# Attention and convolution on one core: the step that turns and scales the next group's minima, at the end of unit 6 in place of the head of unit 7

## The reference

```
q, k, v = t @ Wq.T + bq, t @ Wk.T + bk, t @ Wv.T + bv        # t: (8, 1024, 512), normalised
q, k, v = (z.reshape(B * NUM_HEADS, S, hd) for z in (q, k, v))
scores = einsum('gqd,gkd->gqk', q, k) / sqrt(hd)
wv = einsum('gqk,gkd->gqd', softmax(scores), v)
x = x + wv                                                   # layer 0
x = x + conv3x3(relu(_gn(x) * mask), weight) + bias          # layer 1
```

## Time and profile before

| | |
|---|---|
| median of 3 runs | 2764.5 us (2763.74 to 2767.18) |
| profiled execution | 2762.23 us |
| its span | 2760.4 us |
| mean granted clock of TensorE | 0.976 |
| busy in the span | TensorE 2575.8 us (93%), VectorE 2090.1 (76%), ScalarE 1086.2 (39%), GpSimd 1164.1 (42%) |

### The profile page before, as it was taken

How to read it: one execution, slowest core, us unless ns; L and a number is a source line. 1 busy time by engine, 2 the same in 40 slices (tenths; PEclk the granted TensorE clock), 3 DMA queues, 4 the chain that set the end, 5 groups by cost and what they waited for, 6 DMA issues and landing times.

```text
span 2760.4 us, 39733 instructions
## 1 busy us (share of the span) xinstructions
PE 2575.8 (93%) x11312; PEld 1002.7 (36%) x11312; DVE 2090.1 (76%) x2832; ACT 1086.2 (39%) x1801; POOL 1164.1 (42%) x907
## 2 busy tenths in 40 slices
PE   5989999998999999999899999987599999999998
PEld 2333333333333333333333333322144444444443
DVE  5787788778678778877877877779768968968714
ACT  3444435444454544455444355435323122122100
POOL 3445546655645655565555455564801103003000
PEclk9999999999999999999999999998799999999999
DMA  4233143242433315233331532421154554653524
GB/s 134 67 94 98 46 124 90 61 123 58 107 79 82 101 49 133 69 94 85 90 108 26 143 90 62 118 92 67 62 211 159 181 206 162 233 182 134 198 95 165
DMA packets 209777, 309.10 MB, mean 112 GB/s; under 512 B 80272, under 2 KB 129552, under 8 KB 209552
## 3 DMA queue, kind: packets, MB, share of 16 engines
q1 hardware_dynamic: 209552, 306.36, 36.5%
HBM read 202.88 MB, written 52.69 MB: 93 GB/s over the span
## 4 chain that ended last, share of the span: by engine, by line
PE 77%; DVE 11%; issue 5%; DMA 2%; ACT 2%; POOL 2%; DVEq 0%; SPq 0%; ACTq 0%; POOLq 0%
PE bank L747 27%; PE bank L657 14%; PE bank L602 12%; PE bank L645 11%; PE bank L620 6%; PE bank L612 4%; DVE nmax L1139 3%; DVE prob_sum L1133 2%; PE bank L634 2%; DMA q_b<-shift 1%; DVE val L1156 1%; ACT xn_hi L809 1%; POOL prob_sum L983 1%; DVE nt L209 1%; PE bank L628 0%
## 5 line engine op out<-in xcount | busy, mean ns | idle before, releaser
L1139 DVE TENSOR_REDUCE nmax<-bank 128x1 f32<-128x512 f32 x1024 | 661.2, 683 | 224.6 <-PE bank L620 217.3
L829 ACT ACTIVATE prob<-bank 128x512 f32<-128x512 f32 x1024 | 554.9, 594 | 691.6 <-PE bank L645 665.2
L747 PE MATMUL bank<-v,u_slab 128*128 128x512 f16 x3456 | 749.8, 380 | 3.4 <-DVE v L1307 3.4
L983 POOL TENSOR_TENSOR prob_sum<-prob_sum,prob 128x512 f32<-128x512 f32 x384 | 553.6, 1442 | 439.7 <-ACT prob L829 438.2
L657 PE MATMUL bank<-prob,val 128*64 128x512 f32 x2048 | 520.6, 628 | 2.3 <-ACT prob L829 2.3
L747 PEld LDWEIGHTS bank<-v,u_slab 128*128 128x128 f16 x3456 | 338.8, 98 | 413.4 <-DVE v L1307 5.1
L620 PE MATMUL bank<-k_a,q_a 128*128 128x512 f16 x1024 | 393.6, 388 | 43.8 <-DVE nmax L1139 28.8
L1133 DVE TENSOR_TENSOR prob_sum<-prob_sum,prob 128x512 f32<-128x512 f32 x384 | 380.6, 991 | 24.6 <-DVE shift L1149 16.8
L645 PE MATMUL bank<-q_a,k_a 128*128 128x512 f16 x1024 | 320.6, 385 | 41.3 <-ACT prob L829 40.4
L645 PE MATMUL bank<-q_b,k_b 128*128 128x512 f16 x1024 | 312.2, 387 | 21.3 <-DMA q_b<-shift 21.2
L1034 POOL TENSOR_TENSOR t_a<-tab_mem 128x1224 f32<-128x1224 f32 x16 | 50.1, 3131 | 447.3 <-DVEq L1256 435.0
(11 more groups left out here) (119 smaller groups left out, 2649.2 us busy)
## 6 DMA issues: line engine op xcount, KB each, us to landing
u_slab<-u_scratch SPq DMA_DIRECT2D x72, 1024.0 KB, 5.0
tile<-x_scratch SPq DMA_DIRECT2D x34, 1024.0 KB, 7.5
xs<-x SPq DMA_DIRECT2D x28, 1024.0 KB, 5.8
u_scratch<-u_w SPq DMA_DIRECT2D x96, 192.0 KB, 2.2
q_a<-qk_hi SPq DMA_DIRECT2D x64, 256.0 KB, 5.6
den_sb<-recip_scratch SPq DMA_DIRECT2D x128, 128.0 KB, 2.9
x_scratch<-xr SPq DMA_DIRECT2D x16, 1024.0 KB, 4.9
xr<-x SPq DMA_DIRECT2D x15, 1024.0 KB, 8.7
```

The source lines that it names most:

```text
L747: mm = pe.matmul(bank_at(pos, co)[:].rearrange("p (i n) -> p i n", i=2), slab[:, l, c, co * P:(co + 1) * P], image[v][:, 2 * c:2 * c + 2, ...
L829: act.activation(prob[:, (2 * u + e) % 8], sc_bank[bank_turn(s * 16 + 2 * u + e, 16 * HPI)[0]][:], ACT.Exp, scale=float(D) ** -0.5).then_i ...
L983: nc.gpsimd.tensor_tensor(acc, in0, prob[:, (2 * kc + 1) % 8], ALU.add).then_inc(s1["sum1"], 1)
L1139: dve.tensor_reduce(nmax[:, m // 2, m % 2:m % 2 + 1], src[:], AX.X, ALU.max, negate=True)\
```

## The change

The shift item is moved from place "a" of unit 7 to place "d" of unit 6, ahead of a statistics item if there is one. Both engines and the ring's order follow, since they read the same function; nothing is added or left out.

```
@@ -99,10 +99,10 @@
     tiles = [("max", first + k) for k in range(MAX_QUOTA[u])] if nxt else []
     at = {"a": tiles[0:1], "b": tiles[1:2], "c": tiles[2:]}
     at["d"] = [("value", u // 2)] if v_units and u % 2 else []
+    if nxt and u == UNITS - 2:
+        at["d"].append(("shift", 0))
     if u in stat:
         at["d"].append(("stat", stat.index(u)))
-    if nxt and u == UNITS - 1:
-        at["a"].append(("shift", 0))
     if prev and u == 2:
         at["d"].append(("den", 0))
     return at
```

## The result

The changed kernel takes 2756.49 us in the median (2753.76 to 2761.62), beside 2764.99 for the kernel before (eight runs each). The ratio is 0.9977, with an interval from 0.9967 to 0.9986: about 6.4 us faster, 3.9 to 9.1. The two medians lie 8.5 us apart, inside this interval. The sum of the prediction gave 15.4 us. The time lies inside the predicted range, but the sum is 2.4 times the 6.4 us and 1.8 times the 8.5.

A forecast was written before the change was run, and what follows sets the result against it. Stage 1 was taken as a TensorE stream with a few holes. Gains of 22.1 and 0.65 us less a loss of 7.4 gave 15.4 us off, a median of 2749 us; range 2738 to 2761.

The forecast's parts named there:

- Part 1, slot 2: Slot 2, images 0 to 6: shift ahead of the statistics item ends TensorE's waits; gain 3.16 us per image, 22.1 in all.
- Bounds 1.5 and 2.6: Slot 2's smaller gains per image: 2.6 us if VectorE's chain ends 0.6 later, 1.5 if TensorE's short pieces run at low clock.
- rival (b): Slot 2 gains only 2.6 to 1.5 us per image, 2753 to 2761 us; chance 0.15 up to 2759, beyond it 0.10 shared.
- Right behind 3.1 us of idleness: Slot 2 before the change: granted clock 0.50 from 642.20 to 645.60, following TensorE's waits of 1.76 and 1.32 us.
- Part 2, the wait of slot 7: Slot 7: the shift matmul's wait for the minima holds the value matmuls; loss 1.05 us per image, 7.4 in all.
- Rival (a): Slot 7's stall is taken up by waits TensorE already has there; 2742 us, chance 0.16.
- the clock behind slot 7's wait: Slot 7: no clock fall was put in the sum; with one, 1.7 us more, a bound of 2.75 per image.
- rival (c): Slot 7's stall takes the clock down, 1.7 us more per image; 2761 us, chance 0.10 shared with the smallest slot 2 gains.
- I leave it out of the sum: Low-clock stretches, such as behind slot 3, might be met or missed as phase shifts; some us better or worse, counted as nothing.
- Part 3: Other queues and last image: nothing, except about 0.65 us gained in the last image's slot 5.
- the 5.28 us: Last image, slot 6: TensorE's wait for its row goes, but GpSimd's masks set the end; between 0 and 5, taken as 0.
- (d): Slower: slot 7's wait outweighs slot 2's gain, losing 2.75 against 1.46 us per image with both clocks falling; 2773 us, chance 0.05.

The follow-up runs named there:

- slot 7 alone: Kernel before, with the shift at the end of unit 6 only in slot 7 of images 0 to 6: 2777.61 us, ratio 1.0047.
- the last image alone: Kernel before, with the shift at the end of unit 6 in the last image only: 2763.05 us, ratio 0.9998.
- the filled run: For slot 7: changed kernel, six unread matmuls in its wait, 2746.06 us. For slot 4: changed kernel without slot 7's move, eight in its wait, 2731.22 us.
- cut in two: Changed kernel, but in slot 7 four of the eight value matmuls go ahead of the shift matmul and four behind: 2742.65 us, ratio 0.9918.
- absent: Kernel before, with the shift at the end of unit 6 in all slots but slot 7: 2740.27 us; in slot 2 of images 0 to 6 only: 2741.7 us.
- not filled: Kernel before, with the shift at the end of unit 6 in all slots but slot 7, run again on the slot 4 filling's chip: 2742.55 us.

## Why the prediction was wrong

**Part 1, slot 2, was right.** Forecast -3.16 us per image, measured -3.36 for slots 2 and 3 together. What becomes late next is what was named: VectorE, with six maxima in a row; the first of the six comes 10.53 us behind the start of GpSimd's L989 (631.11 to 641.64), where it was 13.76. The statistics did take to the old end whatever their start: L204 takes 0.51 us instead of 1.00, since it starts later, and the three behind it 1.18 or 1.19 us. GpSimd in the same stretch of the changed kernel:

```profile
631.11 1.27 POOL L989 TENSOR_TENSOR den_sb<-pv_sb,den_sb 128x512 f32<-128x512 f32 x1 [3.44 <-DMA den_sb<-recip_scratch]
632.34 1.26 POOL L983 TENSOR_TENSOR prob_sum<-prob_sum,prob 128x512 f32<-128x512 f32 x1
633.56 1.27 POOL L996 TENSOR_TENSOR xr<-xr,den_sb 128x512 f32<-128x512 f32 x1
634.79 1.26 POOL L983 TENSOR_TENSOR prob_sum<-prob_sum,prob 128x512 f32<-128x512 f32 x1
```

These four operations end at 632.38, 633.60, 634.83 and 636.05; the four held operations of VectorE end at 632.40, 633.63, 634.84 and 636.07. Behind the last of them the same operations take 0.16 us. The Trainium skill (SBUF — State Buffer, "SBUF: two separate sides") calls the port pair that the two engines share an exclusive lock that is held for the whole instruction, on VectorE's side by operations with two inputs in SBUF or in a mode that uses both ports. The trace agrees for L209 and L211; in which mode L204 and L206, with one input, ran is shown nowhere. Bounds 1.5 and 2.6 and with them rival (b) didn't happen: TensorE's short pieces from 639.7 on kept the full clock.

But the size of this gain leans on the old kernel's clock, and here the prediction had luck in its sample. "Right behind 3.1 us of idleness" wasn't a law: in two runs that leave slot 2 as it was (slot 7 alone, the last image alone), the clock stays at full speed behind that pair of waits in 5 of 14 images. TensorE in image 2 of the run with slot 7 alone, and the stretch behind (L622 is a maximum's matmul, L659 the value matmuls):

```profile
647.54 0.39 PE L622 MATMUL bank<-k_a,q_a 128*128 128x512 f16 x1 [1.57 <-DVEq L1154]
649.25 0.61 PE L647 MATMUL bank<-q_b,k_b 128*128 128x512 f16 x2 [1.32 <-DMA q_b<-shift]
649.78 1.94 PE L659 MATMUL bank<-prob,val 128*64 128x512 f32 x8
649.20:652.60 3.40, 3.35 (x15) 1.08 (x16) 2.41 (x4) 1.69 (x3) 0.00 (x0) 1.00 0.89 284
```

In such an image slots 2 and 3 of the old order take 58.9 to 59.1 us, with the low stretch 60.5 to 61.1, and the changed order takes 57.3. So of the 3.36 us about 1.6 are the waits and the rest is a low stretch that the old order met in all seven images of the first profile, and doesn't always meet.

**Part 2, the wait of slot 7, was right in its first term.** Forecast a loss of 1.05 us per image, measured 1.04 where the clock holds (1.03 in the filled run), with a wait of 1.60 us at L628 in all seven images. From the shift matmul to the scores with the row 4.70 us pass, as worked out (778.54 to 783.24). Rival (a) falls: 24.50 against 23.46 us.

**The step that failed is the clock behind slot 7's wait.** I took slot 7's term without a fall of the clock, 7.4 us, and kept 2.75 us per image as a bound; measured is 1.04 in three images and 2.70 in four, 13.9 us together (in other profiles three and four images, and one and six). The price of a fall was right (1.7 forecast, 1.65 measured); that it would come wasn't in the sum. Its grounds were in rival (c): the 1.76 us at 640.25 "alone didn't" take the clock down. That reading was bad: the row after that wait still has full clock, but 1.32 us more of idleness followed at 641.96, and from 642.20 the clock was down. The row proves only that the clock doesn't fall at once, and none of the rows I rested on shows a wait of 1.6 us with full clock long after it. One such row wouldn't have been enough either: in the changed kernel the wait of 1.60 us itself leaves the clock up in three images of seven. Against it stood a hint that I named and didn't weigh: the wait comes soon behind a short one.

**"I leave it out of the sum"** was the second failure. The low stretch "behind slot 3" was named there, without a row, and put at nothing. It lies around the wait of 2.4 us with which slot 4 begins in every image; in image 2 of the kernel before it is 3.4 us at 0.50.

```profile
666.10:669.50 3.40, 3.17 (x8) 0.85 (x10) 3.40 (x4) 2.95 (x6) 3.40 (x4) 0.50 0.25 66
```

Its cost depends on where it begins. Over the images 0 to 6 of all twelve profiles, slot 4 takes 29.90 to 29.92 us without a low stretch (10 times, seven of them filled), 30.72 to 31.49 with one of 3.4 us (58 times), and 32.08 to 32.77 with one of 6.8 us (16 times). A stretch of 3.4 us costs least when it begins 1.4 us ahead of slot 4's scores with the row (30.72), and most when it begins with them or behind (31.43 to 31.49). The wait for the row takes a part of the early ones up: it is 0.15 us in image 2 of before, and 0.59 in the filled run with the clock up. In all seven images of before one of 3.4 us begins 0.5 to 1.4 us ahead of slot 4's scores with the row, and the slot takes 30.75 to 31.15; after, two images have 6.8 us (32.77 and 32.19) and the sum is 4.0 us more. "Up to some us better or worse" was the right size, but not the right middle: in its first profile the kernel before had close to the least that a low stretch costs there, in every image, so moving it could mostly cost. A part of the 4.0 us is chance. In three profiles with the old slot 2 the seven slots 4 sum to 216.4, 218.4 and 218.8 us, in seven with the new one and no filling in slot 4 to 219.1 to 221.5: 2.3 us between the means.

**Part 3 is not contradicted, and no more.** Forecast 0.65 us for the last image, measured 1.1 with stage 2 in one pair of profiles, and in the run that changes the last image alone nothing measurable. From the begin of the last image to the first convolution matmul the four profiles with the old order there take 276.9 to 278.9 us, the eight with the new one 274.8 to 278.0: a term of 0.65 us can't be told in this. That the 5.28 us would come back at GpSimd's masks was right in its result; which engine sets the end there was tested by no run.

**Chances.** Slower by its own mechanism (d) had been priced with both clocks falling and slot 2 at its least. Slot 7 alone does cost 13 us; only the gain of slot 2 outweighs it.

The cause is shown for slot 7 (filled, cut in two, alone, absent) and for slot 4 (filled, not filled). Not shown: what decides in which images the clock falls. It changes between executions of one program, and no run sets it by intent. Nor is it shown whether the wait of 0.26 us shortly before slot 7's plays a part: it is there in every run.

## What to carry to other kernels

When a step is moved ahead in an in-order queue, list what was ready behind it: here eight ready matmuls filled a wait of 1.6 us, and the move was worth 22 us in one slot and cost 13 in another, so it should be made only where its input is already there. Price a new idle gap on TensorE twice, once as the wait and once at half the clock behind it (1.03 and 1.65 us here), unless many gaps of that length in the same kernel, over more than one execution, have full clock long after them; one image is no proof, since the same gap kept the clock in three images here and lost it in four. A gap that can't be closed can be filled with matmuls that nobody reads: it took 11 us off this kernel for one gap per image.

## What the hardware showed that I had not expected

A wait of 1.60 us, with one of 0.26 us shortly before it, brings 1.2 GHz behind it in some images and not in others: four of seven, four of seven, and six of seven in three profiles. Two waits of 1.57 to 1.87 and 1.32 to 1.34 us, with one matmul of 0.39 us between them, did so in 7 of 7 images in one profile of slot 2's old order, in 4 of 7 and 5 of 7 in two others. The same wait filled to 0.30, or cut to 0.59, brought it in none of seven. Around the wait of 2.4 us at slot 4 the clock was down in 74 of 77 images, for 3.4 us or for 6.8, and with the wait filled to 0.66 in none of seven. A clock that falls is not always seen in the row next to the wait: one must look some microseconds further.
